# Attention's value bias ahead of queries and keys, softmax maxima in two halves, negations on ScalarE

## What the reference computes

```
# attention: x is 4 x 32 x 32 x 128, 8 heads of 16 channels, window 7 x 7
qkv  = x @ Wqkv + bqkv
attn = q * 16 ** -0.5 . k_of_the_window + bias          # 49 keys for each query
attn = softmax(attn)
out  = (attn . v_of_the_window) @ Wproj + bproj

# each mixture of experts
logits = x @ gate_w + gate_b
probs  = softmax(logits)                                 # over 8 experts
idx, prb = argmax(probs), max(probs)                     # the token's expert, its weight
kept   = (place of the token among those of its expert) < capacity
y      = (relu(x @ w1[idx] + b1[idx]) @ w2[idx] + b2[idx]) * prb * kept
```

## Time and profile before

| | |
|---|---|
| median of the runs (three shown: 2565.37, 2565.28, 2561.62) | 2565.28 us |
| the profiled execution, its own time | 2566.76 us |
| its span in the trace | 2564.6 us |
| PE, DVE, ACT, POOL busy in it | 2176.9, 2071.5, 1303.8, 1693.2 us |

### The profile page before, as it was taken

One profiled execution on the slowest core, in us unless ns is written; L12 is line 12 of the kernel. 1 busy time (PEld: TensorE's weight loads), 2 busy tenths in 40 slices (PEclk: granted clock), 3 DMA queues, 4 the chain that ended last, 5 costly groups with the idle time before them and its releaser, 6 DMA issues.

```text
span 2564.6 us, 55196 instructions
## 1 busy us (share of the span) xinstructions
PE 2176.9 (85%) x17088; PEld 2051.1 (80%) x17088; DVE 2071.5 (81%) x3905; ACT 1303.8 (51%) x3855; POOL 1693.2 (66%) x1797
## 2 busy tenths in 40 slices
PE   1668798888989888889898888988888889898787
PEld 1467688888888888888898888888888888888777
DVE  4588888888888888888888888888888888887522
ACT  1223355555555555555555555555555555555555
POOL 2677777777777777767777767767777777777000
PEclk6778799999999999999999999999999999999898
DMA  8422222222222222222222222222121111211000
GB/s 189 139 63 60 59 60 65 65 66 64 64 59 56 64 63 63 63 59 64 58 56 65 63 61 63 63 57 57 52 60 55 55 57 56 57 49 58 10 23 4
DMA packets 220186, 157.92 MB, mean 62 GB/s; under 512 B 149994, under 2 KB 187516, under 8 KB 220124
## 3 DMA queue, kind: packets, MB, share of 16 engines
q0 software_dynamic: 55296, 113.36, 15.3%
q1 hardware_dynamic: 163804, 43.50, 7.7%
q10 hardware_dynamic: 1024, 0.26, 0.0%
HBM read 138.67 MB, written 18.04 MB: 61 GB/s over the span
## 4 chain that ended last, share of the span: by engine, by line
PE 61%; DVE 16%; ACT 9%; issue 7%; DMA 3%; SPq 2%; ACTq 1%; DVEq 1%; POOL 0%; POOLq 0%
PE N L1367 15%; PE Z L1460 14%; PE Y L1470 13%; DVE made L909 5%; PE N L1376 4%; ACT prob L1304 3%; ACT hid L1257 3%; DVE got L998 3%; PE N L1539 2%; DMA xt_m<-cold_T 2%; PE N L1532 2%; PE N L1522 2%; ACT L1230 1%; PE N L1514 1%; SPq L662 1%
## 5 line engine op out<-in xcount | busy, mean ns | idle before, releaser
L778 POOL DMA_INDIRECT got<-patches,ranks x1728 | 1677.3, 971 | 637.4 <-issue 491.7
L1257 ACT ACTIVATE hid<-Z,b 128x128 f32<-128x128 f32 x2048 | 580.9, 368 | 307.6 <-PE Z L1460 306.0
L909 DVE TENSOR_TENSOR made<-held,tent 128x1024 f32<-128x1024 f32 x576 | 679.4, 1217 | 46.2 <-PE N L1367 32.3
L1367 PE MATMUL N<-ident,made 128*128 128x128 f32 x4608 | 593.2, 283 | 144.2 <-DVE made L909 140.9
L1367 PEld LDWEIGHTS N<-ident,made 128*128 128x128 f32 x4608 | 529.9, 146 | 179.2 <-DVE made L909 127.1
L1470 PE MATMUL Y<-w,hid 128*128 128x128 f32 x4096 | 577.1, 286 | 50.1 <-ACT hid L1257 50.1
L1460 PE MATMUL Z<-xt_m,w 128*128 128x128 f32 x4096 | 584.1, 291 | 32.4 <-DMA xt_m<-cold_T 32.4
L1460 PEld LDWEIGHTS Z<-xt_m,w 128*128 128x128 f32 x4096 | 543.9, 206 | 45.3 <-DMA xt_m<-cold_T 21.7
L1470 PEld LDWEIGHTS Y<-w,hid 128*128 128x128 f32 x4096 | 524.5, 200 | 65.1 <-ACT hid L1257 56.8
L1003 DVE TENSOR_REDUCE summed<-got 128x32 f32<-128x1152 f32 x192 | 412.7, 2149 | 5.6
L998 DVE TENSOR_TENSOR got<-got,held 128x1152 f32<-128x1152 f32 x192 | 258.5, 1346 | 4.5 <-DMA got<-patches,ranks 0.8
(11 more groups left out here) (204 smaller groups left out, 2239.9 us busy)
## 6 DMA issues: line engine op xcount, KB each, us to landing
got<-patches,ranks POOLq DMA_INDIRECT x1728
vwin<-vpad SPq DMA_DIRECT2D x320, 40.0 KB
patches<-arena SPq DMA_DIRECT2D x92, 96.0 KB
w<-in_L_ffn_w SPq DMA_DIRECT2D x2, 2048.0 KB
patches<-got SPq DMA_DIRECT2D x38, 96.0 KB, 3.0
vpad<-vt SPq DMA_DIRECT2D x128, 16.0 KB
out<-X SPq DMA_DIRECT2D x32, 64.0 KB
xt_m<-cold_T ACTq DMA_DIRECT2D x64, 4.0 KB
```

The costliest lines, as they stand in the source:

```text
L778: pool.indirect_dma_start(out=got[:, q, j * PATCH:(j + 1) * PATCH], out_offset=None, in_=table, in_offset=bass.IndirectOffsetOnAxis(ap=ran ...
L909: v.tensor_tensor(made[:, k % MADE, :].rearrange("p (y x) -> p y x", y=H), across.unsqueeze(2).to_broadcast([P, H, W]), tent[:, 0, k, :].u ...
L1257: ins = a.activation(hid[:, e % 2, c, :], Z[e % 2][:, c * P:(c + 1) * P], ACT.Relu, bias=b1[n][:, e * FC + c:e * FC + c + 1])
L1367: ins = pe.matmul(N[c // 4][:, (c % 4) * P:(c % 4 + 1) * P], made[:, k % MADE, c * P:(c + 1) * P], ident[:, :], start=(k % K == 0 and c % ...
```

## The change

Three things. The value bias (DVE) no longer waits for ACT's keys but for PE's product alone, and ACT's queries wait for the value bias. The maxima of the attention's scores are taken in two halves of 4 blocks, each right behind its bias add. Both negations (routing and attention) move from DVE to ACT, as a copy with scale -1 ahead of the exponentials; in the attention there is one for each half. Two waits of PE follow the new last reader of bank M.

```diff
-        route_v = [Steps(sem(f"route{n}_v"), "stats aggr rstd xn lg max neg eqd first hot rsum pos taken "
+        route_v = [Steps(sem(f"route{n}_v"), "stats aggr rstd xn lg max eqd first hot rsum pos taken "
                          "kept in gate") for n in range(2)]
-        route_s = [Steps(sem(f"route{n}_s"), "std xT exp hot cold") for n in range(2)]
+        route_s = [Steps(sem(f"route{n}_s"), "std xT neg exp hot cold") for n in range(2)]
...
-        att_v = Steps(sem("att_v"), "qbd s0 s1 max neg rsum norm add")
-        att_s = Steps(sem("att_s"), "exp0 exp1 p0 p1 o0 o1")
+        att_v = Steps(sem("att_v"), "qbd s0 max0 s1 max1 rsum norm add")
+        att_s = Steps(sem("att_s"), "neg0 exp0 neg1 exp1 p0 p1 o0 o1")
@@ DVE, route, part logits
                     v.tensor_reduce(small[n][:, 0:1], lg, AX.X, ALU.max).then_inc(*s("max"))
                     v.wait_ge(*d("max", t))
-                    v.tensor_scalar(small[n][:, 1:2], small[n][:, 0:1], -1.0, None, ALU.mult).then_inc(*s("neg"))
@@ DVE, qkv
                 if part == "project":
-                    v.wait_ge(*qkv_s.done("k", t))
+                    v.wait_ge(*qkv_t.done("qkv", t))
                     v.wait_ge(*v_out.through(t - 1))
                     v.tensor_tensor(vt[:, :], M[:, 384:512], bv[:, :], ALU.add).then_inc(*s("v"))
@@ DVE, attend, part scores, in the loop over the two banks k
                         ins.then_inc(*s(f"s{k}"))
-                    v.wait_ge(*d("s1", t))
-                    v.tensor_reduce(soft[:, 0, :], prob, AX.X, ALU.max).then_inc(*s("max"))
-                    v.wait_ge(*d("max", t))
-                    v.tensor_scalar(soft[:, 1, :], soft[:, 0, :], -1.0, None, ALU.mult).then_inc(*s("neg"))
+                        v.wait_ge(*d(f"s{k}", t))
+                        v.tensor_reduce(soft[:, 0, 4 * k:4 * k + 4], prob[:, 4 * k:4 * k + 4, :], AX.X, ALU.max)\
+                            .then_inc(*s(f"max{k}"))
@@ ACT, route, part logits
-                    a.wait_ge(*route_v[n].done("neg", t))
+                    a.wait_ge(*route_v[n].done("max", t))
+                    a.activation(small[n][:, 1:2], small[n][:, 0:1], ACT.Copy, scale=-1.0).then_inc(*s("neg"))
+                    a.wait_ge(*s_done("neg", t))
+                    a.wait_ge(*route_v[n].done("lg", t))
                     a.activation(route_b[n][:, 6, :], route_b[n][:, 0, :], ACT.Exp, bias=small[n][:, 1:2],
                                  accum_out=small[n][:, 3:4]).then_inc(*s("exp"))
@@ ACT, qkv, part project
-                    a.wait_ge(*qkv_t.done("qkv", t))
+                    a.wait_ge(*qkv_v.done("v", t))
@@ ACT, attend, parts scores (half 0) and weights (half 1)
-                    a.wait_ge(*att_v.done("neg", t))
+                    a.wait_ge(*att_v.done(f"max{half}", t))
+                    a.activation(soft[:, 1, 4 * half:4 * half + 4], soft[:, 0, 4 * half:4 * half + 4], ACT.Copy,
+                                 scale=-1.0).then_inc(*s(f"neg{half}"))
+                    a.wait_ge(*att_s.done(f"neg{half}", t))
                     for j in range(4 * half, 4 * half + 4):
@@ PE, route, part turn, n == 1
-                        pe.wait_ge(*qkv_v.done("v", after))
+                        pe.wait_ge(*qkv_s.done("k", after))
```

## The result

The changed kernel takes 2541.4 us (median of 6 runs, 2532.7 to 2546.6) against 2562.4 for the kernel before in the same session: a ratio of 0.9923 (95% interval 0.9896 to 0.9950), 21 us between the medians. The forecast was 2556.3, 9 us faster, with a range of 2534 to 2576. The time lies inside the range but outside the forecast's own 2549 to 2562: it is where rival 1 stands for half of its clock gain (2543). The profiled execution took 2539.08 us, its span 2537.3.

What follows compares the result with a forecast made beforehand. No engine is full; short hand-overs between two stretches of PE bound the kernel. Softmax -31.4, look-up +12.6 and mask +9.8 sum to -9.0 us, giving 2556.3 us, range 2534 to 2576 (the forecast's own 2549 to 2562).

Steps and rivals of the forecast that it cites:

- rival 1: PE's clock stays up in the eleven long slots: 26 us in all, 2530 us; in half of them 2543; chance 0.23.
- The path up to the transposes: In each slot's softmax, PE's transposes come 1.12 us earlier after "spread"; over 28 slots -31.4 us.
- the 0.9 that the prediction named as a sign that it is wrong: At the softmax, transposes coming less than 0.9 us earlier would show the prediction wrong.
- ACT's load behind the copy: In the routing on ACT, the 1.28 us table load moves behind the maximum; first mixture's exponential 1.2 us later.
- rival 4: A table load in the open costs more than its row: look-up 1.28 us more per slot, 2592 us; chance 0.02.
- The wait at the look-up: After the first mixture's routing, PE's look-up starts 0.45 us later in all 28 slots: +12.6 us.
- The mask: At the second mixture, the mask's DMA goes 0.98 us later in ten of 28 slots: +9.8 us.
- Rival 2: Table load costs more than the softmax gives: mask late in all 28 slots (+27.4 us), 2576 us; chance 0.20.
- The sum: Over the slots, -31.4 + 12.6 + 9.8 = -9.0 us, with PE's clock left out.
- The test that the prediction set for itself: Wrong if the count of slots with PE's clock at 0.93 moves by more than three.
- no part of it is PE's speed: From "spread" to PE's transposes it takes 14.7 to 15.1 us in all slots but the first, whatever the clock.
- Without halves the two parts together would give about 0.9: At the softmax, values first and negation on ACT without halved maxima would gain about 0.9 us of the 1.12.

Runs made afterwards that it cites:

- experiment 1: Changed kernel with the negations of both routings back on DVE, all else as changed: 2498.96 us, ratio 0.9754 to the kernel before.
- experiment 7: Changed kernel with the negation back on DVE for the first mixture's routing alone: 2504.2 us, ratio 0.9771 to the kernel before.
- experiment 6: Changed kernel plus one unused exponential ahead of ACT's wait for the routing's maximum, which draws the table load there: 2491.72 us, ratio 0.9731.
- experiment 9: Changed kernel with all negations on DVE, the attention's in halves, values first kept: 2479.45 us, ratio 0.9671 to the kernel before.
- experiment 4: Changed kernel with values first undone; halves and both negations on ACT remain: 2546.5 us, ratio 0.9936 to the kernel before.
- experiment 3: Kernel before with only the value bias moved ahead of queries and keys: 2491.95 us, ratio 0.9733.
- experiment 2: Kernel before with only the routing's negation moved to ACT: 2559.92 us, ratio 1.0001.
- experiment 8: Changed kernel with the negation back on DVE for the second mixture's routing alone: 2511.24 us, ratio 0.9797 to the kernel before.

## Why the prediction was right, and where it was not

The direction and the terms of the path were right; the clock, which the sum left out, was not, nor was the price of a stall of PE.

**The path up to the transposes.** Right in every step: value add at 1.55 us (1.5), half maximum 0.57 (0.57), copy and its wait 0.25 (0.22), first exponential 8.26 (8.3), transposes 13.83 (13.85), in the 16 slots in which PE is not slowed ahead of it. In PE's waits the gain is 33.3 us for 31.4. But the transposes of all 28 slots stand at 14.48 in the mean, for 15.13 before: 0.65 us earlier, under the 0.9 that the prediction named as a sign that it is wrong.

**ACT's load behind the copy.** It stands there as forecast (958.27, 958.57, 959.86). The Trainium skill ("ScalarE: Activation LUTs", What ACT_TABLE_LOAD costs) adds a drain of about 1380 ns to the 1283 of the load. The trace disagrees: the load starts 0.10 us after the copy's end and the exponential 0.01 us after the load's, where the load now stands in the open, and rival 4 is out. The wait at the look-up was 0.45 us in the mean, as taken, but in 19 slots and not 28: 8.6 us for 12.6.

**The mask.** +10.8 us for 9.8 beside the kernel before; beside experiment 1, which differs from the changed kernel in the routing's negations alone, it is 15.1 (29.2 for 14.1). Rival 2 (27) is out in the sum, though experiment 7 shows by its 30.5 us that the wait stays when only the first mixture is mended. That 10.8 came so near 9.8 is in part luck.

**The clock, the step that failed.** The sum says "without the clock", and rival 1 was given 0.23 with at most 26 us. PE's busy time was -28.1 of the -32.6 us in the slots, and the slots came out 23.6 us below the sum's -9.0, nearly all of rival 1's 26. The rows for it were in hand: the transposes behind a pause took 1.94 us for 1.1, and the slots at 0.93 took 2.4 us more. The argument against it was that the clock is also low behind a single pause of 2.39 us elsewhere; but that concerned another place, and said nothing of whether the pauses at the softmax cost something. Filling one of them gave 48 us. The test that the prediction set for itself, a count of slots at 0.93 that moves by more than three, came out against it: thirteen at 0.93 or less became one.

**The stalls' second price.** The look-up's 0.45 us was priced as a wait alone. In twelve slots PE falls to the lower clock behind it, and there the transposes are 0.4 us later than before instead of 1.1 earlier. The prediction had read that the way to the transposes is the same whatever the clock, and "no part of it is PE's speed". That holds for the kernel before, where DVE's maximum (9.6 us behind "spread") comes behind ACT's `relu` (8.05), and also behind a `relu` that PE has slowed (9.6). With the maximum at 7.2 it no longer holds: the `relu`, and so PE's speed, sets the start. Experiments 1 and 6 put the price of the load's place at 43 us beside the rest of the change, for 22.4 forecast. That it came out near the forecast in the end is in part luck: two errors of the clock, one that gave and one that took, and 5.2 us more outside the slots.

**A statement that was wrong.** "Without halves the two parts together would give about 0.9" of the 1.12 us, it said. No run has just these two parts, but the 0.9 does not follow from its own rows: the whole maximum would end at 1056.75 - 1.2 = 1055.55 and one copy for all blocks at about 1055.8, an estimate of 1.3. Values first alone, with the negation on DVE, gives 1.20 and the whole change 1.14. In halves ACT must copy twice, and the second copy lies on its path (0.22 and its wait); it takes what the earlier start gave. With the negation on DVE in halves the gain is 1.60 (experiment 9). Likewise, that the gain falls by 0.4 without values first held for the place (14.28 for 13.83), but not for the time (experiment 4).

**What stays open.** A pause of 0.45 to 0.49 us at the look-up stood in seventeen slots; nine of them went on at the lower clock, and in eight the clock fell later, at the `made` waits. Three more slots were slow there behind pauses of 2.3, 0.27 and 0.1 us. That the pause matters is shown by the runs without it, in which at most the first slot is slow there (experiments 1, 3, 6, 7, 9), against twelve, thirteen, eleven and six with it (the changed kernel, experiments 2, 4 and 8). What decides for a single slot isn't settled, and so neither why experiments 7 and 8 don't add up; which earlier pause decides was not tried apart.

## What to carry to other kernels

A table load is issued with the activation that needs it, so it hides in that activation's wait; an activation that needs no load, put between the wait and it, takes this cover away. Keep such a step on another engine, or draw the load ahead of the wait. Before a path is shortened, ask what stands just behind its last wait: here a `relu` that hangs on PE's speed, hidden until then. Where PE's rows show two durations for the same matmuls, price each pause twice, once as a wait and once by the difference of the two, and try a change's parts singly and together: here values first alone was worth 2.7%, halves with DVE's negations 2.5%, the routing's negation on ACT 0, and the whole change 0.8%.

## What the runs showed of the hardware

Ten unused transposes in a pause of 1.55 us made a kernel 1.8% faster, with the softmax's exponentials and transposes at their old times behind "spread": eight transposes 1.94 us behind the pause, 1.08 behind the filler. PE's granted clock over the 28 slots was 0.95 before and 0.99 with the filler. A pause of 0.45 to 0.49 us at the look-up was followed by matmuls at half speed in nine slots of seventeen; without the pause at most the first slot was slow there. A copy of 128x1 with a scale takes 204 ns on ACT and one of 128x4 212, and a half maximum (128x4 from 400) 0.57 us on DVE for 0.99 of the whole.
